# Two blocks of layernorm, attention and gated feed-forward on one core: swapped head products, scaled attention weights, final additions on GpSimd, rewritten orders

## What is computed

```
xn = layernorm(x)
f  = xn @ W.T + b                                # block 0, attention over 256 rows
s  = softmax(f @ f.T + clip(|i-j|,0,10)*0.01) @ f
g  = silu(shared(xn) + sum of the 2 best of 8 experts(xn), weighted)
x  = x + s * g

xn = layernorm(x)                                # block 1, 8 pairs of sequences, 16 heads of 8
w  = xn @ Wqkv.T
logits = sum over a head's 8 columns of (w / |w|_over_rows)**2 * temp
Pi   = softmax over the 16 heads of logits
dots = sum over rows of Pi/(sum Pi + 1e-8) * w*w
attn = 1 / (1 + dots)
s  = -(w * Pi * attn) @ Wout.T + bout
g  = silu(xn + 0.3 * ((gelu(xn @ W1[e] + b1[e]) @ W2[e] + b2[e]) @ Wo + bo))   # e chosen per pair
x  = x + s * g
```

## Time and profile before

| | before |
|---|---|
| median of 3 runs | 285.0 us (284.75 to 286.66) |
| span of the profiled execution | 284.0 us |
| TensorE busy | 270.9 us, 95% |
| VectorE busy | 223.4 us, 79% |
| ScalarE busy | 203.1 us, 72% |
| GpSimd busy | 157.1 us, 55% |

### The profile page before, as it was taken

One profiled execution on the slowest core, in us unless ns is written; L12 is line 12 of the kernel. 1 busy time (PEld: TensorE's weight loads), 2 busy tenths in 40 slices (PEclk: granted clock), 3 DMA queues, 4 the chain that ended last, 5 costly groups with the idle time before them and its releaser, 6 DMA issues.

```text
span 284.0 us, 6925 instructions
## 1 busy us (share of the span) xinstructions
PE 270.9 (95%) x1974; PEld 238.4 (84%) x1974; DVE 223.4 (79%) x827; ACT 203.1 (72%) x442; POOL 157.1 (55%) x175
## 2 busy tenths in 40 slices
PE   8999999999999989979999999899998999899993
PEld 6566587589998979979999999888997688789893
DVE  4998996998966946435454799975988799989995
ACT  2785776437663585356656697799799599999993
POOL 3100677777777777777776658872655721124200
PEclk9999999999999999999999999999998699999999
DMA  6997011132551111643344572235305772531824
GB/s 199 307 407 247 28 49 59 56 105 77 123 135 47 58 48 59 204 117 110 95 115 131 151 243 73 78 95 172 138 25 163 150 218 71 140 95 26 237 78 146
DMA packets 31221, 36.03 MB, mean 127 GB/s; under 512 B 4792, under 2 KB 24386, under 8 KB 30928
## 3 DMA queue, kind: packets, MB, share of 16 engines
q1 hardware_dynamic: 26864, 27.13, 33.6%
q0 software_dynamic: 4320, 8.47, 8.9%
HBM read 22.97 MB, written 14.12 MB: 131 GB/s over the span
## 4 chain that ended last, share of the span: by engine, by line
PE 56%; ACT 14%; DVE 9%; DMA 8%; issue 8%; POOL 2%; SPq 1%; DVEq 0%; ACTq 0%; POOLq 0%
PE PS L578 10%; PE PS L522 5%; PE PS L508 5%; PE PS L514 5%; PE PS L586 5%; DMA yc_scratch<-YS,XS 5%; PE PS L530 5%; PE PS L549 4%; PE PS L482 3%; PE PS L459 2%; PE PS L564 2%; ACT YS L1950 2%; ACT L1943 2%; PE PS L659 1%; POOL xs_scratch L2382 1%
## 5 line engine op out<-in xcount | busy, mean ns | idle before, releaser
L2405 POOL DMA_INDIRECT yc_scratch<-YS,XS x71 | 74.6, 1051 | 34.7 <-ACT YS L1950 19.3
L578 PE MATMUL PS<-XG,XT 128*128 128x128 f32 x568 | 70.3, 276 | 0.0
L578 PEld LDWEIGHTS PS<-XG,XT 128*128 128x128 f32 x568 | 66.9, 192 | 1.1 <-issue 0.7
L1314 DVE COPY XT<-WE 128x512 f32 x71 | 31.7, 451 | 29.7 <-PE PS L578 28.4
L2382 POOL DMA_INDIRECT xs_scratch<-XA,POS x32 | 32.3, 1008 | 27.2 <-issue 27.2
L586 PE MATMUL PS<-WE,HHE 128*128 x284 | 40.4, 277 | 1.4 <-DVE HHE L1302 1.4
L1943 ACT ACTIVATE EP<-PS 128x256 f32<-128x256 f32 x71 | 27.0, 388 | 20.5 <-PE PS L578 19.2
L586 PEld LDWEIGHTS PS<-WE,HHE 128*128 128x128 f32 x284 | 35.7, 192 | 2.7 <-issue 2.6
L2382 POOL DMA_INDIRECT xs_scratch<-XB,POS x32 | 31.3, 977 | 9.8 <-issue 9.5
L1302 DVE TENSOR_TENSOR HHE<-EP,PS 128x256 f32<-128x256 f32 x71 | 28.7, 412 | 4.5 <-PE PS L586 2.7
L1950 ACT ACTIVATE YS<-PS,XS 128x128 f32<-128x128 f32 x71 | 25.4, 371 | 5.7 <-DMA yc_scratch<-YS,XS 3.7
(11 more groups left out here) (218 smaller groups left out, 571.4 us busy)
## 6 DMA issues: line engine op xcount, KB each, us to landing
XS<-xs_scratch SPq DMA_DIRECT2D x71, 65.0 KB
XB<-yc_scratch SPq DMA_DIRECT2D x8, 512.0 KB, 4.2
WE<-in_we SPq DMA_DIRECT2D x1, 3072.0 KB, 14.5
X<-in_x SPq DMA_DIRECT2D x8, 256.0 KB, 5.1
out<-X SPq DMA_DIRECT2D x8, 256.0 KB, 2.2
S<-wf_scratch SPq DMA_DIRECT2D x7, 257.0 KB, 2.8
XB<-wf_scratch SPq DMA_DIRECT2D x6, 257.0 KB, 3.5
yc_scratch<-YS,XS POOLq DMA_INDIRECT x71, 2.5
```

What stands on the lines that cost most here:

```text
L578: m = e.matmul(PS[k][:, f * 128:(f + 1) * 128], WC[:, u % 4, f * 128:(f + 1) * 128], XG[:, g % 2, j * 128:(j + 1) * 128], start=True, stop ...
L1314: e.tensor_copy(WC[:, u % 4, :], WE[:, bass.ds(reg[u // 4][u % 4], 512)]).then_inc(s_wc, 1)
L2405: e.indirect_dma_start(out=yc, out_offset=bass.IndirectOffsetOnAxis(ap=XS[:, g % 4, j, 128:129].bitcast(U32), axis=0), in_=YS[:, u % 8, :] ...
```

## The change

1. `heads(c)` swaps its operands: HB, padded with zeros to 32 columns, is the stationary operand and F's 128 columns move. The four products write to partitions 0, 32, 64 and 96 of one bank. ScalarE's new `heads` copies the bank to HT, TensorE's new `turn_h` transposes HT, and `center` reads that.
2. `weigh_out` and WOB are gone. `attn_out` multiplies by attn as well, so it now stands behind `attention`, and `out1` uses Wout itself.
3. `end_x` of chunks 0 to 6 is done by GpSimd; chunk 7's stays on VectorE as `end_v` with a semaphore of its own.
4. All five lists are in a new order. SP's `load_w2` (1 MB) moved from behind `fetch(15)` to behind `fetch(34)`, and `fetch(65)` to `fetch(70)` now stand behind three `collect`.

```diff
-        RB = sb("RB", [128, 400])
+        RB = sb("RB", [128, 512])
+        HT = sb("HT", [128, 2, 128])
...
-        HB = RB[:, 0:256].rearrange("p (b h) -> p b h", h=16)
+        HB = RB[:, :].rearrange("p (b h) -> p b h", h=32)
...
-        WOB = EP[:, 1, :].rearrange("p (b d) -> p b d", d=128)
...
             def store(c):
-                e.wait_ge(s_end, c + 1)
+                e.wait_ge(*((s_ends_v, c - 6) if c >= 7 else (s_end, c + 1)))
...
                 for i in range(4):
-                    m = e.matmul(PS[k][:, i * 16:(i + 1) * 16], F[:, 4 * c + i, 0:128], HB[:, 2 * c + i // 2, :],
+                    m = e.matmul(PS[k][32 * i:32 * i + 32, 0:128], HB[:, 2 * c + i // 2, :], F[:, 4 * c + i, 0:128],
                                  start=True, stop=True)
                 m.then_inc(p_hd, 1)
+
+            def turn_h(c, k, free=None, n=0):
+                e.wait_ge(s_ht, c + 1)
+                when(free, n)
+                e.transpose(PS[k][:, 0:128], HT[:, c % 2, :], ident).then_inc(p_ht, 1)
...
             def out1(c, k, free=None, n=0):
-                e.wait_ge(s_wob, c + 1)
                 e.wait_ge(s_ot, 2 * c + 2)
...
-                    m = e.matmul(PS[k][:, i * 128:(i + 1) * 128], tile(WT, 4 * c + i), WOB[:, (2 * c + i // 2) % 8, :],
+                    m = e.matmul(PS[k][:, i * 128:(i + 1) * 128], tile(WT, 4 * c + i), d_("wout"),
...
             def center(c, k):
-                lg = PS[k][:, 0:64].rearrange("p (i h) -> p i h", i=4)
-                e.wait_ge(p_hd, c + 1)
+                lg = PS[k][:, 0:128].rearrange("p (i h) -> p i h", i=4)[:, :, 0:16]
+                e.wait_ge(p_ht, c + 1)
...
                 e.wait_ge(s_w, b // 2 + 1)
-                e.tensor_tensor(w, pi(k), w, ALU.mult).then_inc(s_ot, 1)
+                e.wait_ge(s_attn, b // 2 + 1)
+                e.scalar_tensor_tensor(out=w, in0=pi(k), scalar=ATT[:, b:b + 1], in1=w, op0=ALU.mult, op1=ALU.mult).then_inc(s_ot, 1)
...
+            def heads(c, k):
+                e.wait_ge(p_hd, c + 1)
+                e.activation(HT[:, c % 2, :], PS[k][:, 0:128], ACT.Copy, bias=0.0, scale=1.0).then_inc(s_ht, 1)
+
             def soft(c):
...
-            def weigh_out(c):
-                e.wait_ge(s_attn, c + 1)
-                if c >= 4:
-                    e.wait_ge(p_o1, c - 3)
-                for b in (2 * c, 2 * c + 1):
-                    m = e.activation(WOB[:, b % 8, :], d_("wout"), ACT.Copy, bias=0.0, scale=ATT[:, b:b + 1])
-                m.then_inc(s_wob, 1)
...
+            def end_x(c):
+                e.wait_ge(s_gs, c + 1)
+                e.tensor_tensor(four(X, c), four(X, c), four(F, c), ALU.add).then_inc(s_end, 1)
```

More of the change, by code:

```diff
@@ L413, in _ @@
             fetch(64)
+            collect(3)
+            store_w2(0)
+            collect(4)
+            collect(5)
             fetch(65)
@@ new lines, in _ @@
+            down_e(65, 5, s_hhe, 67)
+            gate_up(70, 1, s_ys, 64)
+            down_e(66, 5, s_ys, 66)
+            turn_h(0, 6, s_hhe, 68)
+            down_e(67, 0, s_w, 3)
+            heads(1, 3)
+            down_e(68, 4)
+            down_e(69, 6)
+            turn1(3, 5, s_ys, 67)
+            heads(2, 7)
+            down_e(70, 0, s_ys, 68)
+            turn_h(1, 2)
+            turn1(4, 1)
+            proj(3, 3)
+            turn_h(2, 6)
+            spread(0, 2, s_ctr, 2)
+            spread(1, 5)
@@ new lines, in _ @@
+            turn1(5, 7)
+            ff_up(0, 1, s_xt1, 5)
+            proj(4, 0)
+            spread(2, 7, s_xt1, 6)
+            proj(5, 3)
+            spread(3, 6, s_ctr, 3)
+            choose1(1, 4)
+            ff_up(1, 2, s_ot, 1)
+            heads(3, 5, s_ot, 2)
+            spread(4, 4, s_a1, 2)
+            ff_out(0, 1)
+            spread(5, 3, s_w, 6)
+            heads(4, 0)
+            choose2(1, 2)
+            turn_h(3, 6, s_ot, 4)
+            ff_up(2, 7)
+            ff_out(1, 1)
@@ new lines, in _ @@
+            ff_up(3, 6, s_ctr, 4)
+            ff_up(4, 5)
+            turn_h(4, 2)
+            ff_out(2, 7)
+            ff_out(3, 7)
+            heads(5, 0)
+            ff_up(5, 5, s_h1, 5)
+            ff_out(4, 4, s_ot, 5)
+            ff_up(6, 7, s_t, 2)
+            ff_up(7, 2)
+            ff_up(8, 6)
+            ff_out(5, 4)
+            ff_out(6, 0)
+            spread(6, 3, s_ot, 6)
+            turn_h(5, 2, s_h1, 8)
+            ff_out(7, 0)
+            ff_up(9, 7)
+            turn1(6, 5)
@@ new lines, in _ @@
+            spread(7, 4)
+            ff_up(10, 2, s_ctr, 6)
+            turn1(7, 1)
+            ff_out(8, 6)
+            proj(6, 5)
+            choose1(2, 7)
+            spread(8, 1)
+            spread(9, 3, s_ot, 7)
+            ff_out(9, 6)
+            choose2(2, 2)
+            out1(0, 4, s_ot, 8)
+            out1(1, 0)
+            proj(7, 2, s_neg, 3)
+            out1(2, 7)
+            out1(3, 4, s_gs, 1)
+            spread(10, 0, s_gs, 2)
+            heads(6, 3, s_ot, 10)
+            out1(4, 1)
@@ new lines, in _ @@
+            ff_up(11, 6)
+            ff_up(12, 4, s_gs, 4)
+            spread(11, 5, s_w, 7)
+            heads(7, 3, s_ht, 7)
+            ff_out(10, 7)
+            ff_out(11, 7)
+            turn_h(6, 6)
+            turn_h(7, 4, s_h1, 13)
+            out1(5, 1)
+            ff_up(13, 5)
+            ff_out(12, 0)
+            spread(12, 7, s_t, 6)
+            spread(13, 6)
+            ff_up(14, 3)
+            ff_up(15, 1, s_gs, 6)
+            ff_out(13, 0)
+            spread(14, 4)
@@ L1800, in _ @@
-            attention(1)
-            dots(5, 2)
-            attn_out(5, 2)
+            sel_logits(1, 2)
+            center(3, 6)
+            dots(5, 3)
+            select(1)
+            attention(2)
+            share(3)
+            ff_out(0, 1)
+            add_results(6)
+            add_results(7)
+            add_shared(6)
+            add_shared(7)
+            attn_out(4, 4)
+            center(4, 2)
+            ff_out(1, 7)
             gate_s(6)
-            center(5, 5)
+            gate_s(7)
@@ L1805, in _ @@
             gate_x(6)
-            gate_s(7)
+            attn_out(5, 3)
+            gate_x(7)
             stats1(6)
-            gate_x(7)
-            ff_out(1, 3)
             stats1(7)
-            ff_out(2, 2)
+            ff_out(2, 4)
             norm1(6)
+            center(5, 2)
             norm1(7)
-            dots(6, 6)
-            attn_out(6, 6)
+            dots(6, 3)
+            share(4)
             dots(7, 4)
+            attention(3)
+            attn_out(6, 3)
+            ff_out(3, 0)
@@ L1833, in _ @@
+            attention(4)
+            share(5)
+            select(2)
+            end_s(0, 4)
+            weigh(6)
+            end_s(1, 0)
+            attn_out(8, 1)
+            attn_out(9, 3)
+            end_s(2, 7)
+            end_s(3, 4)
+            weigh(7)
+            dots(10, 0)
+            end_s(4, 1)
+            dots(11, 5)
+            attention(5)
+            attn_out(10, 0)
+            attn_out(11, 5)
+            center(6, 6)
+            center(7, 4)
             share(6)
-            select(2)
+            ff_out(5, 7)
```

1731 lines of the change are left out of this document (812 added, 919 removed).

## The result

The kernel after takes 294.2 us (median of four), the kernel before beside it 285.6. The ratio is 1.031, with a 95% interval of 1.026 to 1.035: slower by 3%, where 280.6 was forecast.

The account below looks back on a forecast made before the run. TensorE was taken to bound the kernel up to the tail, VectorE and ScalarE the tail. Hand-over -1.4, table loads -0.5 and tail -2.5 make -4.4 from 284.0: span 279.6, median 280.6 us; range 276.5 to 285.5.

Parts of the forecast that it names:

- The tail, VectorE: Last stretch: seven end_x and one collision go, waits on GpSimd's additions come; -2.5 us, bounds -5.2 and +1.1.
- the port takes the gain back: Rival, chance 0.14: each of seven GpSimd additions holds up a VectorE step in the tail, +6.3 us; 284.2 us.
- The hand-over: From rows to results, where experts begin: earlier GpSimd DMAs and later load_w2 remove TensorE waits; -1.4 us, bounds 0 and -2.5.
- Table loads: ScalarE has 40 instead of 42, 1.28 us each; the one fewer ahead of the tail gives -0.5 us.
- The tail, ScalarE: Last stretch: weigh_out and one table load go, heads copies come; -4.3 us, bounds -2.4 and -5.0.
- The tail, TensorE: Last stretch: heads at 0.89 us plus a transpose adds 1.0 us, taken by 8 us of slack.
- the column groups do run side by side: Rival, chance 0.20: the four products of heads run in parallel, heads and turn_h 0.33 us a chunk; 278.8 us.
- SP's queue: Rival, chance 0.16: fetch(65) waits behind three collect and store_w2(0), delaying TensorE's last turn_x, +4.0 us; 284.6 us.
- The slower rival: Rival, chance 0.08: the passes of heads don't overlap, +1.7 us a chunk on TensorE; 290.5 us.

Follow-up runs that it names:

- The run with cut additions: Kernel after with chunk 6's final addition on VectorE and GpSimd's additions cut to 8 of 128 columns: 281.0 us, ratio 0.983.
- without the drain: Kernel after with the final addition of chunk 6 kept on VectorE, right behind its end_s: 288.3 us, ratio 1.013.
- the run on the kernel before: Kernel before with load_w2 alone moved from behind fetch(15) to behind fetch(34): 285.83 us against 285.88, ratio 1.000.

## Why the prediction was wrong

*The end of GpSimd's list* is the step that failed first: no term of the sum stands for it. The prediction counted the final addition of chunk 6 on GpSimd as 1.18 us; as that list's last instruction it costs 1.18 + 9.2 us to the program's end. The row that shows this, a drain of 10.37 us, was in the trace of before, where it ended at 279.3, four microseconds short of mattering. It accounts for 6.2 of the 7.5 us by which the span grew.

*The tail, VectorE*, was mis-sized: -2.5 told, 58.75 to 61.25 measured, +2.5. The mechanism was as told (a step in SBUF held while GpSimd adds), the size was not: three new collisions of 0.9, +2.7, against +6.4 measured on the five lines above. The sum looked only at the seven moved additions. With all of these on VectorE the five lines still take 9.8 us against 7.3: some 2.5 of the 6.4 come from `add_bias`, which was there before and now meets `attention`, and 3.9 from the moved additions. The rearranged order was part of the change, and I priced it at nothing. A smaller term at nothing was the second multiplication of `attn_out`: its steps went from 418 to 474 ns, 0.9 us for sixteen, and the run without it gives VectorE 1.1 us back.

The run with cut additions, 281.0 us, is near the forecast's 280.6, and in part by luck: it leaves out nearly all of GpSimd's additions, and with the same cut the kernel before has 284.4. Compared so, the new order is ahead by 1.1% (0.983 to 0.994), about 3 us. With the additions cut that much gain is there; whole, they take it back in waits. The rival "the port takes the gain back" had the right mechanism with 284.2 us; without the drain it came to 288.3.

*The hand-over*, -1.4, was nothing, its own bound of 0, and for the reason named there: `positions` waits 0.89 us for TensorE's product `ranks`, which came at 26.50 us in the kernel after. `disp(0)` started at 30.24, not 28.6; `scat(0)`, at 110.14 instead of 113.03, came earlier, mostly by its new place ahead of two DMAs of 1.28. And the wait behind the 1 MB load moved with it, as the run on the kernel before shows.

*Table loads*, -0.5, were not tried by themselves. There are 40 as told, but from 217.8 us on both traces have 17, so that the tail lost one is not seen.

*The tail, ScalarE*: 39.29 of 40 fell to 34.07, but in the whole stretch it is 57.15 to 54.58, -2.6 where -4.3 was told and -2.4 was the bound. The 16 copies of `weigh_out` took their 5.3 with them, seven new copies take 2.0 (1.9 told), and the table load didn't go. It doesn't end the tail any more.

*The tail, TensorE*: `heads` was to take 0.89, and takes 0.43. Eight passes of 128 columns with pitches of 0.11 can't end in that time one after another (7 x 0.11 + 0.28 = 1.05), so the column groups do run side by side. That rival's mechanism is right. Its gain does not show in the time; that VectorE hides it is argued, not tried. The Trainium skill, "TensorEngine Tiling (Array Packing)", section "Key Properties", says that tiles operate independently; the trace agrees (0.43 us). The drain on a change of tiling mode that it also names is not apart in these rows.

*SP's queue*: the 1.69 us wait came, at 202.29, not the 3.9 of the rival, but taking it away gave nothing that can be told. *The slower rival* (passes that don't overlap) did not come about; slower it was, by a mechanism that none of the rivals had.
